# Turning queries and keys of self-attention: TensorE transposes against transposing DMA transfers

## Chip, cores and metric

The kernel runs on one core of a Trainium2 chip. The metric is the device time of one launch in microseconds, as the median of several runs. One execution is also taken by the hardware profiler; its page and its trace are what is read below. PE is TensorE (PEld its weight loads), DVE is VectorE, ACT is ScalarE, POOL is GpSimd, SP is SyncE, and SPq is SyncE's DMA queue.

## What is computed

Two decoder layers on x of shape (2, 1024, 256), with a context of 77 rows. The part that matters is layer 0's self-attention, with 16 heads of 16 channels:

```
q = quat_norm(quat_linear(x, qW, qb))
k = quat_norm(quat_linear(x, kW, kb))
v = quat_linear(x, vW, vb)
scores = einsum('bthd,bshd->bhts', q, k) * scale + mean(sin(J)) * 0.1
out = quat_linear(einsum('bhts,bshd->bthd', softmax(scores), v), oW, ob)
```

After it come a memory attention over the context, a feed-forward of 8 experts, and layer 1 (a long convolution, a cross-attention, and a feed-forward with quantised weights). Each is added to x and normalised.

## The kernel before

Each engine has its own instruction stream, written out by hand, with semaphores between them. The 2,048 rows are 16 tiles of 128 (T = 16, TB = 8 for each batch).

**Projections** (L853 to L882 on VectorE, L1386 to L1422 on TensorE). For each tile t, TensorE turns x and projects queries, keys and values. VectorE adds the bias (`biased`, L766), then, for a tile two steps back, takes the reciprocal of the norms and scales (`normed`, L773 and L775), and splits each value into a high and a low float16 part (`low_part`, L786 and L787). GpSimd adds pairs of squares and the bias of the values, and at the end a bias to x (L362).

**Self-attention** goes by UN = 16 units, each two heads of one batch. A unit has 8 steps `kt`, one for each tile of 128 keys. `stage(u)` on VectorE copies the unit's queries (L805) and keys (L810) out of QKH into QS and KS: 128 rows in partitions, and for each of 8 tiles 128 float16 values (2 heads x 4 parts x 16 channels). TensorE turns each tile (`turn_q`, L1331; `turn_k`, L1340) into bank 7, and VectorE copies the bank to QT and KT (`turned_q`, L820; `turned_k`, L824). QS, KS, QT and KT have two buffers each.

TensorE's order in a unit: at each step the next two `scores` (L1352; three ahead of the exponentials, in six banks), then `values` (L1366), then at steps 0 and 1 the turns of the next unit's queries, and at steps 3 and 4 those of its keys. ScalarE takes one exponential of 128x1024 for each `scores` (L518). VectorE's order in unit u (`attn_unit`): stage unit u+1, the two copies of turned tiles, in units 1 to 9 a part of the quantisation of the last weights (L834 to L840), then the copy of the unit's output out of bank 6 (L850). Unit 0's turns stand inside the projections, the queries' after tile 12 and the keys' after tile 14, and their copies at t = 14 and t = 15.

**SyncE** issues nearly all DMAs in one order. After the loads of the last weights it waits for each third of their quantisation, stores it to w_kept (L292), loads two experts (L284, L285), waits until the keys of the last unit are staged (L296), and then loads the weights of layer 1 (L298 and on).

Of the kernel before, what the change touches and what calls it, by code (L numbers as in the profile page):

```python
# [7 lines left out]
F16 = mybir.dt.float16  # L8
# [8 lines left out]
P = 128  # L17
B, L, D = 2, 1024, 256
T = B * L // P
TB = T // B  # L20
# [3 lines left out]
UN = B * NP  # L24
# [24 lines left out]

LN_CN = tuple(range(LN_C, LN_C + E - 2)) + (LN_C + E, LN_C + E + 3)  # L50
LN_DN = (LN_CN[6] - 2, LN_CN[6] - 1, LN_CN[7] - 2, LN_CN[7] - 1) + tuple(range(LN_CN[7] + 1, LN_E))

TURN_Q = {0: range(0, 4), 1: range(4, 8)}
TURN_K = {3: range(0, 4), 4: range(4, 8)}

UX = T * KD
AHEAD = 3
# [14 lines left out]
def decoder(nc, a, out):  # L72
    w_kept = nc.dram_tensor("w_kept", (P, 18, D), F32, kind="Internal").ap()
    with ExitStack() as ctx:
        sems = {}

        def sem(name):
            if name not in sems:
                sems[name] = ctx.enter_context(nc.semaphore(name))
            return sems[name]  # L80
# [171 lines left out]
        def bank(n, dt=F32):  # L252
            v = PS[:, n, :]
            return v if dt == F32 else v.bitcast(dt)
# [6 lines left out]
        def _(sp):  # L261
# [21 lines left out]
            def load_expert(e):  # L283
# [3 lines left out]
            sp.dma_start(wq[:, 6:12], a["L1_ffn_w_up"].rearrange("(k p) d -> p k d", p=P)).then_inc(sem("w_up_raw"), 16)  # L287
            sp.dma_start(wq[:, 12:18].rearrange("p (k c) d -> p k (c d)", k=KD),
                         a["L1_ffn_w_down"].rearrange("(k p) i -> p k i", p=P)).then_inc(sem("w_down_raw"), 16)
            for n in range(3):  # L290
                sp.wait_ge(sem("w_deq"), n + 1)
                sp.dma_start(w_kept[:, 6 * n:6 * n + 6], wq[:, 6 * n:6 * n + 6]).then_inc(sem("w_kept"), 16)  # L292
            sp.wait_ge(sem("w_kept"), 16 * 3)
            load_expert(0)
            load_expert(1)
            sp.wait_ge(sem("ks"), UN)  # L296
            for i, w in enumerate(("L1_attn_W_proj", "L1_xattn_Wq", "L1_xattn_Wk", "L1_xattn_Wv")):
                sp.dma_start(l1raw[i], a[w].rearrange("(k p) d -> p k d", p=P)).then_inc(sem("l1_w_in"), 16)  # L298
            for i, w in enumerate(("L1_attn_b_proj", "L1_attn_gamma", "L1_attn_beta", "L1_xattn_bo")):
# [422 lines left out]
        def _(dve):  # L722
# [69 lines left out]
            def stage(u):  # L792
                w = u % 2
                if u == 0:
                    dve.wait_ge(sem("j_exp"), 1)
                    dve.wait_ge(sem("const"), 9)
                    dve.wait_ge(sem("v_biased"), TB)
                    dve.wait_ge(sem("qk_lo"), TB)
                    for v in range(2):
                        ins = dve.tensor_scalar(VS[v][:, :, :, DH:DH + 1], ones[:, 0:1, None, None].to_broadcast([P, TB, 2, 1]), ec, None, ALU.mult)  # L800
                    link(ins)
                if u >= 2:
                    dve.wait_ge(sem("q_tr"), u - 1)
                for s in range(4):
                    ins = dve.tensor_copy(QS[w][:, :, :, s, :], QKH[:, 0, u, :, s // 2, :].rearrange("p t (h d) -> p t h d", h=2))  # L805
                ins.then_inc(sem("qs"), 1)
                if u >= 2:
                    dve.wait_ge(sem("k_tr"), u - 1)
                for s in range(4):
                    ins = dve.tensor_copy(KS[w][:, :, :, s, :], QKH[:, 1, u, :, s % 2, :].rearrange("p t (h d) -> p t h d", h=2))  # L810
                ins.then_inc(sem("ks"), 1)
                if u >= 2:
                    dve.wait_ge(sem("pv_done"), TB * (u - 1))
                dve.tensor_scalar(VS[w][:, :, :, 0:DH], VV[:, u].rearrange("p t (h d) -> p t h d", h=2), ec, None, ALU.mult).then_inc(sem("vs"), 1)

            def turned_q(u):
                dve.wait_ge(sem("q_tr"), u + 1)
                if u >= 2:
                    dve.wait_ge(sem("qk_done"), 2 * TB * (u - 1))
                dve.tensor_copy(QT[u % 2], bank(7, F16)).then_inc(sem("qt"), 1)  # L820

            def turned_k(u):
                dve.wait_ge(sem("k_tr"), u + 1)
                dve.tensor_copy(KT[u % 2], bank(7, F16)).then_inc(sem("kb"), 1)  # L824

            def quantised(n, part):

# [14 lines left out]
            def attn_unit(u):  # L842
                if u + 1 < UN:
                    stage(u + 1)
                    turned_q(u + 1)
                    turned_k(u + 1)
                if 1 <= u <= 9:
                    quantised((u - 1) // 3, (u - 1) % 3)
                dve.wait_ge(sem("pv_done"), TB * u + TB)
                dve.tensor_copy(OSB[:, u], bank(6)).then_inc(sem("o_evac"), 1)  # L850

            for t in range(T + 3):
                if t < T:  # L853
                    biased(t)
                if t == T - 2:
                    turned_q(0)
                if t == T - 1:
                    turned_k(0)
                if t == 4:
                    mask()  # L860

# [437 lines left out]
        def _(pe):  # L1299
# [22 lines left out]
                mm.then_inc(sem("v_mm"), 1)  # L1322


            def turn_q(u, tiles):
                if 0 in tiles:
                    pe.wait_ge(sem("qs"), u + 1)
                    if u >= 1:
                        pe.wait_ge(sem("kb"), u)
                for k in tiles:  # L1330
                    mm = pe.transpose(bank(7, F16)[:, P * k:P * k + P], QS[u % 2][:, k].rearrange("p h s d -> p (h s d)"), ident16)  # L1331
                if TB - 1 in tiles:
                    mm.then_inc(sem("q_tr"), 1)

            def turn_k(u, tiles):
                if 0 in tiles:
                    pe.wait_ge(sem("ks"), u + 1)
                    pe.wait_ge(sem("qt"), u + 1)
                for k in tiles:
                    mm = pe.transpose(bank(7, F16)[:, P * k:P * k + P], KS[u % 2][:, k].rearrange("p h s d -> p (h s d)"), ident16)  # L1340
                if TB - 1 in tiles:
                    mm.then_inc(sem("k_tr"), 1)

            def scores(n):

                u, kt, half = n // (2 * TB), n // 2 % TB, n % 2
                if n % (2 * TB) == 0:
                    pe.wait_ge(sem("kb"), u + 1)
                if n >= 3:
                    pe.wait_ge(sem("exp_done"), n - 2)  # L1350
                for h in range(2):
                    mm = pe.matmul(bank(2 * (n % 3) + h), KT[u % 2][64 * h:64 * h + 64, P * kt:P * kt + P],  # L1352
                                   QT[u % 2][64 * h:64 * h + 64, 512 * half:512 * half + 512], start=True, stop=True)
                mm.then_inc(sem("qk_done"), 1)
# [15 lines left out]
            def attn_unit(u):  # L1370
                for kt in range(TB):
                    for n in range(2 * (TB * u + kt) + 3, 2 * (TB * u + kt) + 5):
                        if n < 2 * TB * UN:
                            scores(n)
                    values(u, kt)
                    if u + 1 < UN:
                        if kt in TURN_Q:
                            turn_q(u + 1, TURN_Q[kt])
                        if kt in TURN_K:
                            turn_k(u + 1, TURN_K[kt])  # L1380


            x_turn(0)
# [2 lines left out]
            for t in range(T):  # L1386
# [29 lines left out]
                                           start=(k == 0), stop=(k == KD - 1))  # L1416
                    mm.then_inc(sem("mem_g_mm"), 1)

                if t == TB + 4:
                    turn_q(0, range(TB))  # L1420
                if t == T - 2:
                    turn_k(0, range(TB))  # L1422

            pe.wait_ge(sem("qk_biased"), T)
            pe.wait_ge(sem("v_evac"), T)
# [414 lines left out]
```

## Time and profile before

| | us |
|---|---|
| median of 3 runs | 878.62 (876.58 to 883.43) |
| the profiled execution, its own time | 880.1 |
| its span, first to last instruction | 878.3 |
| PE busy | 764.4 (87%) |
| ACT busy | 553.1 (63%) |
| DVE busy | 543.4 (62%) |
| POOL busy | 188.3 (21%) |
| mean granted TensorE clock | 0.951 of full speed |

The busy shares are over the whole span, and the stages differ. A busy PE is not PE at its peak: matmuls are pipelined, and their modelled ends overlap. The questions to ask of each stage are which engine has no gaps, and what the others wait for.

### The profile page before, as it was taken

To read this page: it belongs to the slowest core of one execution; us is meant where nothing else is said; L and a number is where in the kernel's file an instruction comes from. 1 tells how busy PE (TensorE), PEld (TensorE's weight loads), DVE (VectorE), ACT (ScalarE), POOL (GpSimd) and SP (SyncE) were. 2 spreads that over 40 slices of the span, in tenths; PEclk is the share of its full clock that TensorE was granted. 3 is DMA by queue.
4 is the path that set the end of the run, shared out by engine and by line. 5 is a ranking of instruction groups with operands and counts; after the bars stand their busy time and mean duration, and the time that the engine had idled before them with its cause. 6 is when DMAs were issued, how large, how long until landed. Compare 5 with 4: busy or idle time off the path is not lost.

```text
span 878.3 us, 11330 instructions
## 1 busy us (share of the span) xinstructions
PE 764.4 (87%) x4105; PEld 446.5 (51%) x4105; DVE 543.4 (62%) x1120; ACT 553.1 (63%) x941; POOL 188.3 (21%) x214
## 2 busy tenths in 40 slices
PE   4974899999999989999699999679899979994397
PEld 2642122222222228988588888346556844441286
DVE  4899334342412118869821647878977567898886
ACT  3555799999999981423221341475777533598991
POOL 1678000000000002306000402384544200000002
PEclk9997899999999999999899999889999989998599
DMA  7200000000150220202053200002000000000002
GB/s 204 91 0 1 1 1 37 1 37 1 42 188 1 70 69 1 96 1 97 1 192 114 78 1 1 0 1 72 10 28 1 1 1 0 1 0 0 1 24 72
DMA packets 23582, 33.76 MB, mean 38 GB/s; under 512 B 3074, under 2 KB 20328, under 8 KB 23400
## 3 DMA queue, kind: packets, MB, share of 16 engines
q1 hardware_dynamic: 23384, 32.92, 11.3%
q8 instruction: 33, 0.54, 0.3%
q14 instruction: 21, 0.17, 0.1%
q10 hardware_dynamic: 144, 0.13, 0.1%
HBM read 28.59 MB, written 4.46 MB: 38 GB/s over the span
## 4 chain that ended last, share of the span: by engine, by line
PE 39%; ACT 31%; DVE 21%; issue 6%; POOL 1%; SPq 1%; DMA 1%; DVEq 0%; POOLq 0%; ACTq 0%
ACT arena L518 24%; PE banks L1812 5%; PE banks L1804 5%; PE banks L1605 5%; PE banks L1593 5%; PE banks L1705 3%; PE banks L1677 2%; DVE arena L893 2%; DVE arena L901 2%; DVE arena L1185 2%; PE banks L1502 2%; DVE arena L773 1%; ACT arena L695 1%; ACT arena L681 1%; PE banks L1625 1%
## 5 line engine op out<-in xcount | busy, mean ns | idle before, releaser
L518 ACT ACTIVATE arena<-banks 128x1024 f32<-128x1024 f32 x256 | 236.3, 1060 | 10.0 <-PE banks L1352 7.5
L1366 PE MATMUL banks<-arena 128*32 128x512 f32 x1024 | 138.1, 611 | 2.3 <-ACT arena L518 0.8
L342 POOL TENSOR_SCALAR arena<-arena 128x2 f32<-128x2 f32 (+1 forms) x38 | 10.0, 263 | 474.1 <-DVE arena L896 474.1
L1352 PE MATMUL banks<-arena 64*128 64x512 f16 x512 | 89.3, 389 | 11.9 <-ACT arena L518 8.0
L1804 PE MATMUL banks<-arena 128*128 128x512 f32 x192 | 85.9, 610 | 3.8 <-DVE arena L1196 3.7
L609 ACT ACTIVATE arena<-banks,arena 128x77 f32<-128x77 f32 x256 | 58.9, 363 | 22.1 <-DVE arena L1109 22.1
L1352 PEld LDWEIGHTS banks<-arena 64*128 64x128 f16 x512 | 22.9, 93 | 95.9 <-ACT arena L518 78.1
L1812 PE MATMUL banks<-arena 128*128 128x256 f32 x192 | 44.5, 397 | 26.6 <-ACT arena L716 26.6
L1804 PEld LDWEIGHTS banks<-arena 128*128 128x128 f32 x192 | 37.4, 196 | 51.7 <-issue 48.7
L1605 PE MATMUL banks<-arena 128*128 128x256 f32 x256 | 58.1, 389 | 5.8 <-DVEq L1031 5.8
L1605 PEld LDWEIGHTS banks<-arena 128*128 128x128 f32 x256 | 49.9, 196 | 13.1 <-issue 6.2
L1593 PE MATMUL banks<-arena 128*128 128x256 f32 x256 | 56.2, 380 | 0.0
L1812 PEld LDWEIGHTS banks<-arena 128*128 128x128 f32 x192 | 38.5, 201 | 33.0 <-ACT arena L716 27.4
L421 POOL TENSOR_TENSOR arena<-arena 128x616 f32<-128x616 f32 x32 | 42.2, 1320 | 59.6 <-DVE arena L1117 59.5
L824 DVE COPY arena<-banks 128x1024 f16<-128x1024 f16 x16 | 11.0, 690 | 70.4 <-PE banks L1340 70.4
L901 DVE TENSOR_SCALAR arena<-arena 128x256 f32<-128x256 f32 x96 | 45.5, 527 | 13.1 <-POOL arena L344 13.0
L1677 PE MATMUL banks<-arena 128*128 128x308 f32 x128 | 43.1, 462 | 11.5 <-ACT arena L609 8.4
L1593 PEld LDWEIGHTS banks<-arena 128*128 128x128 f32 x256 | 48.7, 190 | 6.4
L579 ACT ACTIVATE arena<-banks,arena 128x256 f32<-128x256 f32 x64 | 26.2, 473 | 39.9 <-PE banks L1593 39.8
L850 DVE COPY arena<-banks 128x512 f32<-128x512 f32 x16 | 11.1, 691 | 64.7 <-PE banks L1366 64.7
L675 ACT ACTIVATE arena<-banks 128x512 f32<-128x512 f32 x48 | 28.1, 609 | 36.0 <-PE banks L1804 36.0
L535 ACT ACTIVATE arena<-banks 128x1024 f32<-128x1024 f32 x18 | 18.5, 1028 | 44.6 <-PE banks L1475 38.8
(221 smaller groups left out, 1407.4 us busy)
## 6 DMA issues: line engine op xcount, KB each, us to landing
arena<-in_L_ffn_w SPq DMA_DIRECT2D x16, 1024.0 KB, 7.4
w_kept<-arena SPq DMA_DIRECT2D x3, 768.0 KB, 3.3
arena<-w_kept SPq DMA_DIRECT2D x3, 768.0 KB, 5.1
arena<-in_x SPq DMA_DIRECT2D x4, 512.0 KB, 8.1
out_x<-arena SPq DMA_DIRECT2D x3, 512.0 KB, 2.9
arena<-in_L_ffn_b SPq DMA_DIRECT2D x1, 1024.0 KB, 9.0
arena<-in_L_ffn_w_gate SPq DMA_DIRECT2D x1, 768.0 KB, 7.4
arena<-in_L_ffn_w_up SPq DMA_DIRECT2D x1, 768.0 KB, 9.1
```

The costliest lines, as they stand in the source:

```text
L421: pool.tensor_tensor(Ex[n % 4], Ex[n % 4], rdx[:, n % 4, :, None].to_broadcast([P, HC, LC]), ALU.mult).then_inc(sem("xa_w"), 1)
L518: act.activation(PT[kt % 2][:, half], PS[:, 2 * (n % 3):2 * (n % 3) + 2, :], ACT.Exp, scale=DH ** -0.5 / QK_UP ** 2).then_inc(sem("exp_don ...
L609: ins = act.activation(Ex[n % 4][:, h, :], PS[:, 2 * (n % 2) + h // 4, LC * (h % 4):LC * (h % 4) + LC], ACT.Exp, scale=-1.0, bias=mxs[:, 8 ...
L675: act.activation((GF if n < IC * G4 else UF)[:, c, 512 * g:512 * g + 512], bank(2 + n % 4), ACT.Copy).then_inc(sem("gu"), 1)
L901: ins = dve.tensor_scalar(dst(j), src(j), mv[:, at + j, 0:1], rstd[:, at + j:at + j + 1], ALU.subtract, ALU.mult)
L1352: mm = pe.matmul(bank(2 * (n % 3) + h), KT[u % 2][64 * h:64 * h + 64, P * kt:P * kt + P], QT[u % 2][64 * h:64 * h + 64, 512 * half:512 * h ...
L1366: mm = pe.matmul(PS[32 * j:32 * j + 32, 6, :], VS[w][:, kt, h, :], PT[kt % 2][:, half, h, :], start=(kt == 0), stop=(kt == TB - 1))
L1593: mm = pe.matmul(PS[:, f // 2, 256 * (f % 2):256 * (f % 2) + 256], W1r[r][:, k, P * f:P * f + P], XT[:, k, TE * P * e:TE * P * e + TE * P] ...
L1605: mm = pe.matmul(bank(4 + e % 2)[:, D * j:D * j + D], hT[e % 2][:, f, P * j:P * j + P], W2r[r][:, f, :], start=(f == 0), stop=(f == FT - 1))
L1677: mm = pe.matmul(PS[:, 2 * (n % 2) + q, 0:4 * LC], qTx[g % 2][:, k, P * j:P * j + P], Kbd[:, k, g // 2, 4 * q:4 * q + 4, :].rearrange("p h ...
L1804: mm = pe.matmul(bank(2 + n % 4), (wgT if n < IC * G4 else wuT)[:, k, P * c:P * c + P], XT[:, k, 512 * g:512 * g + 512], start=(k == 0), s ...
L1812: mm = pe.matmul(PS[:, t % 8 // 2, D * (t % 2):D * (t % 2) + D], UF[:, c, P * t:P * t + P], wdT[:, c, :], start=(c == 0), stop=(c == IC - 1))
```

## The change

The turns on TensorE and the copies out of bank 7 go. In their place SyncE issues two DMA transfers a unit, SBUF to SBUF, that transpose: QS to QT and KS to KT, 128 x 1024 float16 each. For unit u it waits until queries are staged, until the transfer of the unit before has landed, and until the scores of unit u-2 are done; then, after the first is issued, until keys are staged. TensorE waits for both transfers (of 16 counts each) ahead of the first scores of a unit. VectorE waits for the transfer of unit u-2, where it waited for its turns, before it writes the staging buffer again. SyncE's stores to w_kept stand behind the transfers of units 5, 8 and 11, and the loads of experts 0 and 1 behind those of unit 12. The loads of layer 1's weights wait until the last transfers have landed.

```diff
-            for n in range(3):
-                sp.wait_ge(sem("w_deq"), n + 1)
-                sp.dma_start(w_kept[:, 6 * n:6 * n + 6], wq[:, 6 * n:6 * n + 6]).then_inc(sem("w_kept"), 16)
-            sp.wait_ge(sem("w_kept"), 16 * 3)
-            load_expert(0)
-            load_expert(1)
-            sp.wait_ge(sem("ks"), UN)
+            def turned(u):
+
+                sp.wait_ge(sem("qs"), u + 1)
+                if u >= 1:
+                    sp.wait_ge(sem("q_turned"), 16 * u)
+                if u >= 2:
+                    sp.wait_ge(sem("qk_done"), 2 * TB * (u - 1))
+                sp.dma_start(QT[u % 2].rearrange("p (k n) -> p k n", k=TB), QS[u % 2].rearrange("p k h s d -> p k (h s d)"),
+                             transpose=True).then_inc(sem("q_turned"), 16)
+                sp.wait_ge(sem("ks"), u + 1)
+                if u >= 1:
+                    sp.wait_ge(sem("k_turned"), 16 * u)
+                sp.dma_start(KT[u % 2].rearrange("p (k n) -> p k n", k=TB), KS[u % 2].rearrange("p k h s d -> p k (h s d)"),
+                             transpose=True).then_inc(sem("k_turned"), 16)
+
+            for u in range(UN):
+                turned(u)
+                if u in (5, 8, 11):
+                    n = (u - 5) // 3
+                    sp.wait_ge(sem("w_deq"), n + 1)
+                    sp.dma_start(w_kept[:, 6 * n:6 * n + 6], wq[:, 6 * n:6 * n + 6]).then_inc(sem("w_kept"), 16)
+                if u == 12:
+                    sp.wait_ge(sem("w_kept"), 16 * 3)
+                    load_expert(0)
+                    load_expert(1)
+            sp.wait_ge(sem("q_turned"), 16 * UN)
+            sp.wait_ge(sem("k_turned"), 16 * UN)
...
                 if u >= 2:
-                    dve.wait_ge(sem("q_tr"), u - 1)
+                    dve.wait_ge(sem("q_turned"), 16 * (u - 1))
...
                 if u >= 2:
-                    dve.wait_ge(sem("k_tr"), u - 1)
+                    dve.wait_ge(sem("k_turned"), 16 * (u - 1))
...
-            def turned_q(u):
-                dve.wait_ge(sem("q_tr"), u + 1)
-                if u >= 2:
-                    dve.wait_ge(sem("qk_done"), 2 * TB * (u - 1))
-                dve.tensor_copy(QT[u % 2], bank(7, F16)).then_inc(sem("qt"), 1)
-
-            def turned_k(u):
-                dve.wait_ge(sem("k_tr"), u + 1)
-                dve.tensor_copy(KT[u % 2], bank(7, F16)).then_inc(sem("kb"), 1)
...
                     stage(u + 1)
-                    turned_q(u + 1)
-                    turned_k(u + 1)
...
-                if t == T - 2:
-                    turned_q(0)
-                if t == T - 1:
-                    turned_k(0)
...
                 if n % (2 * TB) == 0:
-                    pe.wait_ge(sem("kb"), u + 1)
+                    pe.wait_ge(sem("q_turned"), 16 * u + 16)
+                    pe.wait_ge(sem("k_turned"), 16 * u + 16)
...
                     values(u, kt)
-                    if u + 1 < UN:
-                        if kt in TURN_Q:
-                            turn_q(u + 1, TURN_Q[kt])
-                        if kt in TURN_K:
-                            turn_k(u + 1, TURN_K[kt])
...
-                if t == TB + 4:
-                    turn_q(0, range(TB))
-                if t == T - 2:
-                    turn_k(0, range(TB))
```

The functions `turn_q` and `turn_k` on TensorE go with them.

## Rows read from the trace of the kernel before

**Rows 1.** Busy time of each engine in three stretches; here self-attention (stretch, length, engines).
```profile
79.00:327.00 248.00, 230.50 (x1770) 57.13 (x1770) 79.71 (x204) 236.86 (x258) 9.04 (x4) 0.97 0.12 40
```

**Rows 2.** Chain of waits in self-attention (start us, length us, what).
```profile
104.65 1.70 ACT arena L518 x2
...
178.37 1.70 ACT arena L518 x2
...
311.05 1.70 ACT arena L518 x2
...
323.80 2.10 ACT arena L518 x2
```

**Rows 3.** Timeline of ACT in unit 0 (start us, length us; in brackets idle before, releaser).
```profile
79.60 3.75 ACT L518 ACTIVATE arena<-banks 128x1024 f32<-128x1024 f32 x4
84.17 1.02 ACT L518 ACTIVATE arena<-banks 128x1024 f32<-128x1024 f32 x1 [0.83 <-PE banks L1366]
92.69 1.02 ACT L518 ACTIVATE arena<-banks 128x1024 f32<-128x1024 f32 x1 [7.49 <-PE banks L1352]
95.07 2.02 ACT L518 ACTIVATE arena<-banks 128x1024 f32<-128x1024 f32 x2 [1.35 <-PE banks L1366]
97.39 2.85 ACT L518 ACTIVATE arena<-banks 128x1024 f32<-128x1024 f32 x3 [0.30 <-PE banks L1366]
```

**Rows 4.** Timeline of all engines, unit 0 and a step of unit 6.
```profile
90.81 0.63 DVE L805 COPY arena<-arena 128x256 f16<-128x256 f16 x4
91.36 0.62 DVE L810 COPY arena<-arena 128x256 f16<-128x256 f16 x4
...
91.50 0.61 PE L1331 MATMUL banks<-arena 128*128 128x128 f16 x4 [7.46 <-DVE arena L805]
...
93.00 1.94 PE L1366 MATMUL banks<-arena 128*32 128x512 f32 x8
...
182.28 0.61 PE L1352 MATMUL banks<-arena 64*128 64x512 f16 x4
182.82 1.06 PE L1366 MATMUL banks<-arena 128*32 128x512 f32 x8
```

**Rows 5.** Timeline of DVE in the projections: the bias additions.
```profile
53.34 0.68 DVE L766 TENSOR_TENSOR arena<-banks,arena 128x512 f32<-128x512 f32 x1
...
56.66 0.68 DVE L766 TENSOR_TENSOR arena<-banks,arena 128x512 f32<-128x512 f32 x1
...
62.39 0.67 DVE L766 TENSOR_TENSOR arena<-banks,arena 128x512 f32<-128x512 f32 x1
...
73.34 0.68 DVE L766 TENSOR_TENSOR arena<-banks,arena 128x512 f32<-128x512 f32 x1
```

**Rows 6.** A stretch of 3 us in unit 0; the granted clock stands third from last.
```profile
92.00:95.00 3.00, 3.00 (x16) 0.47 (x15) 0.25 (x1) 1.02 (x1) 0.00 (x0) 0.50 0.01 3
```

**Rows 7.** Timeline of DVE after the start of unit 6.
```profile
180.12 0.69 DVE L850 COPY arena<-banks 128x512 f32<-128x512 f32 x1 [2.42 <-PE banks L1366]
180.72 0.62 DVE L805 COPY arena<-arena 128x256 f16<-128x256 f16 x4
181.26 0.63 DVE L810 COPY arena<-arena 128x256 f16<-128x256 f16 x4
```

**Rows 8.** Small loads: SP's timeline, DMA issues (KB, us to landing), queue from 4 to 6.
```profile
0.79 1.39 SPq L264 DMA_DIRECT2D arena<-in_L_attn_qW  x2
...
4.85 1.27 SPq L264 DMA_DIRECT2D arena<-in_L_attn_oW  x2
...
arena<-in_L_attn_oW SPq DMA_DIRECT2D x2, 64.0 KB, 2.4
...
q1 hardware_dynamic: 863, 0.21, 45.6%
```

**Rows 9.** DMA issues from 180 to 350 us: KB each, median us to landing.
```profile
arena<-in_L_ffn_w SPq DMA_DIRECT2D x4, 1024.0 KB, 9.9
...
arena<-in_L_attn_W_proj SPq DMA_DIRECT2D x1, 256.0 KB, 2.9
```

More of the change, by code:

```diff
@@ L51 @@
 LN_DN = (LN_CN[6] - 2, LN_CN[6] - 1, LN_CN[7] - 2, LN_CN[7] - 1) + tuple(range(LN_CN[7] + 1, LN_E))
-TURN_Q = {0: range(0, 4), 1: range(4, 8)}
-TURN_K = {3: range(0, 4), 4: range(4, 8)}
 UX = T * KD
@@ L1322, in project @@
                 mm.then_inc(sem("v_mm"), 1)
[L1325 to L1342, printed above, removed]
             def scores(n):
```

## Prediction

> **What bounds the kernel now.** I read the busy shares by stage first. Self-attention runs from 79 to 327 us; ScalarE is busy in 236.9 of its 248.0 us, PE in 230.5, VectorE in 79.7 [rows 1]. Its work is 256 exponentials, 16 a unit (L518). The chain of waits stands on them from start to start: the pair at 104.65 opens unit 1, the pair at 178.37 unit 6, and the pair at 311.05 unit 15, which is 14.74 us a unit [rows 2]. Unit 15, in which PE turns nothing, has its eight pairs from 311.05 to 323.80 in seven steps, 12.75 us, so 14.57 us a unit [rows 2]. ScalarE's timeline then shows where it stands idle: only in unit 0, for 0.83, 7.49, 1.35 and 0.30 us, 9.97 in all [rows 3]. The long one is the thing to see. PE stands at its first turn of unit 1 (L1331) until VectorE has staged queries (L805, ending at 91.44); the next scores are queued behind that turn, so ScalarE gets no banks to read [rows 4]. VectorE is late because it still finishes the projections.
>
> **What goes.** In units 1 to 14, 16 turns each leave PE, and two copies out of bank 7 leave VectorE. The turns made ScalarE's pace 14.74 instead of 14.57, so (14.74 - 14.57) x 14 = 2.4 us come back. The copies lie beside ScalarE's work and give nothing themselves.
>
> In the projections VectorE sets the pace: three of its bias additions L766 follow that of 62.39 by 73.34, 3.65 us each, against 3.32 undisturbed (53.34 to 56.66) [rows 5]. The excess of 1.0 us is unit 0's turns and the copy L820, so the last bias addition comes 1.0 us earlier, and the first exponential at 78.6 instead of 79.60. VectorE itself gains the second copy as well, 0.6 us by the bank copy L850, next of kin [rows 7], which puts the staging of unit 1 at 89.84 (queries) and 91.98 - 1.6 = 90.38 (keys) [rows 4].
>
> The 7.49 us wait goes, since PE no longer waits for staging in the middle of unit 0. PE remains cold at that point. After the idle stretch eight value matmuls took 1.94 us against 1.06 later [rows 4]; the granted clock there was 0.50, which is 1.2 GHz, against a mean of 0.97 over the stage, nearly always 2.4 GHz [rows 1, 6]. So I keep 1.5 of the other 2.48 us. The earliest start of unit 1 is 78.6 + 14.57 + 1.5 = 94.7, a gain of 10.0 against 104.65.
>
> **What comes.** Each unit has two transfers of 256 KB on SyncE's queue. PE waits for both in front of the first scores of the unit, and behind that wait are queued the values of step 6 and two more pairs of scores. After landing, ScalarE needs one pair of scores and one step of values: 0.6 + 1.1 = 1.7 us [rows 4]. In a running unit, VectorE first copies the output of the last one (L850, 180.12), then has queries staged at 181.34 and keys at 181.89, which is 2.97 and 3.52 us after the unit's start at 178.37 [rows 2, 7]. Queries cannot be staged earlier, since that copy stands ahead of them. So with a fixed latency F and a time T in the DMA engines for each transfer, a unit lasts at least 2.97 + F + 2T + 1.7. The bar is 14.74.
>
> F: 64 KB in 256 pieces of 256 bytes land 2.4 us after issue [rows 8]. In a stretch of only such pieces 863 took 45.6% of 16 engines x 2 us, so 16.9 ns each in one engine [rows 8], and 256 of them 0.27 us. I take F = 2.0, rounded down from 2.1. The bar is then passed at T = 4.0.
>
> T: no row shows a transposing transfer. Its source is 1,024 runs of 256 bytes. If it moves like a plain one, T is 1,024 x 16.9 / 16 ns = 1.1 us. If every value is written on its own, it is 131,072 x 16.9 / 16 ns = 138 us. These are the two ends. Neither is likely: neighbours in a source row go to different partitions, which speaks against the first, and the second is a hundred times the price of any row. With no row nearer to either, I take the geometric middle, 12.2 us, pieces of some 11 values. Pieces of 16 values would give 8.7.
>
> The Trainium skill, page "VectorE: DVE Perf Modes", section "The three transpose paths", gives 1309 ns for one 128x128 turn by DMA against 390 ns on TensorE. Eight such blocks are, as an estimate, 10.5 us, and the sum below would give 1094. No run so far shows either figure.
>
> With T = 12.2 the first keys land at 89.84 + 2.0 + 24.4 = 116.2 and unit 1 starts at 117.9, 13.3 late. PE has then been idle and is cold, for which I add the restart stalls of 1.35 + 0.30 = 1.65 [rows 3]: 14.9. The following 14 starts are 2.97 + 2.0 + 24.4 + 1.7 + 1.65 = 32.7 us apart, 18.0 over 14.74, or 252. The gain of 2.4 and the start's 10.0 are swallowed by it. Sum: 880.1 + 14.9 + 252 = 1147 against the profiled execution's own time; that one lies 1.5 us above the median of 878.62, so **1146**.
>
> **Edits that I cost at nothing.** The stores to w_kept move behind the turns of units 5, 8 and 11; nobody waits for them but the expert loads. These four loads of 1 MB land after 9.9 us at the median [rows 9] and are issued behind the turns of unit 12. On a 14.7 us unit they are over before unit 13's turns. At 32.7 us the more so. If they overlapped they would add up to 10 us once. The eleven loads of layer 1's weights now wait for the last turns. None is larger than an expert's, their readers come after attention, and unit 15's own 14.57 us cover them.
>
> **Rivals.** *One: transfers as quick as plain ones.* A 256 KB load landed in 2.9 us [rows 9], so keys could land 0.54 + 2.9 after queries are staged, at 93.3. The eight 64 KB loads, 2,048 pieces of 256 bytes like one unit's two transfers, took 7.1 us from 0.79 to about 7.9, which puts it at 96.9 [rows 8]. Both lie within the 14.74 of a running unit, and then nothing waits after unit 1; that holds up to T = 4.0. Midway, 5.3 us, unit 1 starts at 96.8, 7.8 earlier than before; with the 2.4 it is 10.2, so 869.9 profiled and 868.4. The ends are 866 and, without the 2.4, 873. For it speaks that every row of the queue shows quick pieces; against, that no row shows a value leaving its run. The Trainium skill, page "Advanced Engine Details and Errata", section "X-Bar Transpose (TRN2)", says that transposing DMAs are as fast as regular ones, which is this rival; the trace so far has none to hold beside it.
>
> *Two: a price for each block.* If each of the 16 blocks of 128x128 costs what a small DMA costs in the queue, 7.1 / 8 = 0.89 us [rows 8], keys land 14.2 us after queries are staged. Unit 1 then starts at 89.84 + 14.2 + 1.7 + 1.65 = 107.4, 2.7 late, and the other 14 starts are 20.5 us apart, 5.8 over: 81. That is 880.1 + 84 - 1.5 = 963. For it: SyncE was held 0.6 to 0.7 us for each small load [rows 8]. Against: 256 KB in one piece landed in 2.9 us, hardly later than 64 KB in 2.4 [rows 8, 9], so bytes or blocks cost little there.
>
> *Three: the cold clock alone.* PE loses the turns and may be granted less in running units. Unit 15 speaks against it: without turns it kept its pace. It is in the range of rival one.
>
> **How the numbers follow.** Forecast (T above 7.3, times from 1000 on) 0.45; rival two and T between 4 and 7.3 together 0.18; rival one 0.37. One per cent is 8.8 us, about what can be told from no change: below 869.8 is faster. Of rival one's 0.37 I put 0.23 below it and 0.14 within; slower gets 0.63. The forecast's own range is 1000 to 1250: T = 15.7, some nine values to a piece. It reaches no further, since 0.12 is left above. As cases of both signs hold most of the chance, the range for 8 in 10 has to take in rival one from 866: **866 to 1250**.
>
> **What would show it.** Right: in the list of waits ScalarE's L518 waits for scores (L1352) or values (L1366) 15 times, some 18 us at a time; PE's granted clock is near 0.5 after each; PE's scores wait for a DMA from arena to arena; the landing time of the second transfer of a unit is about 26 us. Right in any case: the 7.49 us wait is gone and the first exponential starts near 78.6. Wrong: a landing time of both below 9 us from the staging of queries, starts of units 14.6 us apart, unit 1 starting near 97. If landing is short but SyncE's own issue is long, T is the sequencer's and not the engines'; the sum is the same.

## The result: one per cent faster, where 30% more time was forecast

The changed kernel takes **869.8 us** (median of 12 runs, 868.4 to 873.9) against 879.1 of the kernel before beside it (12 runs, 876.3 to 884.0). The ratio is 0.9899, with a 95% interval of 0.9885 to 0.9913. The prediction said 1146 and slower. What happened is its first rival, which gave 868.4, and 869.9 for the profiled execution; that took 869.56 around a span of 867.8.

ScalarE's timeline in unit 0 answers to [rows 3] (start, length, in brackets the idle time before it and its releaser; L535 is the line L518 of before, L1349 the values L1366, L1335 the scores L1352):

```profile
77.89 3.75 ACT L535 ACTIVATE arena<-banks 128x1024 f32<-128x1024 f32 x4
82.45 1.94 ACT L535 ACTIVATE arena<-banks 128x1024 f32<-128x1024 f32 x2 [0.82 <-PE banks L1349]
85.29 9.27 ACT L535 ACTIVATE arena<-banks 128x1024 f32<-128x1024 f32 x10 [0.90 <-PE banks L1349]
95.89 16.61 ACT L535 ACTIVATE arena<-banks 128x1024 f32<-128x1024 f32 x18 [1.32 <-PE banks L1349]
```

The wait of 7.49 us is gone. The two waits for values that stood around it are now 0.82 and 0.90, and one is new, 1.32 us where unit 1 starts. After that row ScalarE runs through. The busy time of the page by line says the same for all 256 exponentials (busy, mean ns, then idle before and its releaser):

```profile
L535 ACT ACTIVATE arena<-banks 128x1024 f32<-128x1024 f32 x256 | 235.4, 1094 | 3.1 <-PE banks L1349 3.0
```

The timeline of all engines shows the new path, where [rows 4] had a turn on PE waiting for VectorE's copies:

```profile
89.13 0.64 DVE L822 COPY arena<-arena 128x256 f16<-128x256 f16 x4
...
89.68 0.63 DVE L827 COPY arena<-arena 128x256 f16<-128x256 f16 x4
89.79 1.23 SPq L294 DMA_TRANSPOSE arena<-arena  x1
...
91.12 1.27 SPq L299 DMA_TRANSPOSE arena<-arena  x1
...
94.37 0.39 PE L1335 MATMUL banks<-arena 64*128 64x512 f16 x2 [1.71 <-DMA arena<-arena]
```

Queries are staged at 89.77, their transfer holds SyncE's queue for 1.23 us, the keys' transfer follows, and PE's first scores of unit 1 go 4.6 us after the staging. The chain of waits puts a length on the keys' transfer, 3.15 us (start, length, what):

```profile
91.12 3.15 DMA arena<-arena
94.28 0.09 issue
94.37 0.39 PE banks L1335 x2
94.76 1.04 PE banks L1349 x8
```

In the DMA view of 98 to 118 us, four transfers of running units (packets, MB, share of 16 engines; then the issues with the median us to landing):

```profile
q1 hardware_dynamic: 4224, 1.05, 27.4%
...
arena<-arena SPq DMA_TRANSPOSE x4, 3.2
```

A transfer is 1,056 packets. 27.4% of 16 engines x 20 us over 4,224 packets is 20.8 ns each, so a transfer keeps the 16 engines for 1,056 x 20.8 / 16 ns = 1.37 us. This is the prediction's T, for which it took 12.2.

**Where the 10.5 us of the profiled spans went** (878.3 to 867.8). From the bias addition of 56.66 [rows 5] to the first exponential it was 22.94 us and is now 22.06 (55.83 to 77.89): 0.9. The first exponential came 1.7 earlier, so the other 0.8 lies ahead of those tiles, in a stretch that the change does not touch. Unit 0 lasted 25.05 us (79.60 to 104.65) and lasts 18.00: 7.05. Units 1 to 14 took 206.4 [rows 2] and take 205.6 (95.89 to 301.48): 0.8. Unit 15 is the same, seven steps in 12.75 us (the chain: 301.48 to 314.23). After attention 552.4 us became 551.5, which lies within the 550.1 to 553.0 of the other kernels here. What the change can claim of it is 0.9 + 7.05 + 0.8, some 8.8, beside 9.3 between the medians.

### The profile page after: what moved, and what is told of

Same layout as the page of the kernel before. It is cut to its first block, busy times and chain, and to the rows that moved or that the text cites. A ratio compares the mean times of both kernels' runs of the same rounds, so it can differ in the third digit from the quotient of the medians.

```text
span 867.8 us, 10805 instructions
## 1 busy us (share of the span) xinstructions
PE 752.1 (87%) x3849; PEld 431.9 (50%) x3849; DVE 522.2 (60%) x1088; ACT 552.0 (64%) x941; POOL 191.5 (22%) x214
## 4 chain that ended last, share of the span: by engine, by line
PE 38%; ACT 30%; DVE 21%; issue 7%; DMA 1%; SPq 1%; POOL 1%; DVEq 0%; POOLq 0%; ACTq 0%
ACT arena L535 24%; PE banks L1786 5%; PE banks L1778 5%; PE banks L1579 5%; PE banks L1567 5%; PE banks L1679 3%; PE banks L1651 2%; DVE arena L894 2%; DVE arena L902 2%; DVE arena L1186 2%; PE banks L1476 2%; DVE arena L790 2%; ACT arena L712 1%; ACT arena L698 1%; PE banks L1599 1%
## 5 line engine op out<-in xcount | busy, mean ns | idle before, releaser
L535 ACT ACTIVATE arena<-banks 128x1024 f32<-128x1024 f32 x256 | 235.4, 1094 | 3.1 <-PE banks L1349 3.0
L1349 PE MATMUL banks<-arena 128*32 128x512 f32 x1024 | 138.1, 611 | 2.2 <-ACT arena L535 0.8
L1335 PE MATMUL banks<-arena 64*128 64x512 f16 x512 | 99.4, 390 | 23.1 <-ACT arena L535 9.4
L359 POOL TENSOR_SCALAR arena<-arena 128x2 f32<-128x2 f32 (+1 forms) x38 | 12.7, 334 | 462.2 <-DVE arena L897 462.2
L1335 PEld LDWEIGHTS banks<-arena 64*128 64x128 f16 x512 | 24.7, 93 | 166.8 <-ACT arena L535 154.4
L1786 PEld LDWEIGHTS banks<-arena 128*128 128x128 f32 x192 | 38.4, 200 | 33.1 <-ACT arena L733 27.4
L894 DVE BATCH_NORM_STATS2 arena<-arena 128x6 f32<-128x256 f32 x112 | 40.2, 414 | 1.2
```

The costliest lines, as they stand in the source:

```text
L535: act.activation(PT[kt % 2][:, half], PS[:, 2 * (n % 3):2 * (n % 3) + 2, :], ACT.Exp, scale=DH ** -0.5 / QK_UP ** 2).then_inc(sem("exp_don ...
L894: ins = dve.bn_stats(bstat[:, at + j, :], view(j))
L1349: mm = pe.matmul(PS[32 * j:32 * j + 32, 6, :], VS[w][:, kt, h, :], PT[kt % 2][:, half, h, :], start=(kt == 0), stop=(kt == TB - 1))
L1786: mm = pe.matmul(PS[:, t % 8 // 2, D * (t % 2):D * (t % 2) + D], UF[:, c, P * t:P * t + P], wdT[:, c, :], start=(c == 0), stop=(c == IC - 1))
```

## The experiments

Two questions were open. Does the gain need the DMA at all, or is it only the end of PE's wait in unit 0 (theory A), against work taken off PE and VectorE in every unit (theory B)? And what do the transfers cost, by which the prediction fell? Medians, ratios to the kernel before on the same chip and what ScalarE did in attention (from the first exponential to the end of the last, and idle within it, from its timeline):

| kernel | us | ratio, 95% interval | attention | idle | unit 1 starts after the first exponential |
|---|---|---|---|---|---|
| before | 879.1 | 1 | 246.3 | 9.97 | 25.05 |
| changed | 869.8 | 0.9899 (0.9885 to 0.9913) | 238.4 | 3.04 | 18.00 |
| turns of unit 1 later, all on PE | 869.9 | 0.9898 (0.9878 to 0.9918) | 238.4 | 2.13 | 17.19 |
| GpSimd later, kernel before | 871.3 | 0.9918 (0.990 to 0.9935) | 239.6 | 3.38 | |
| both of these, no DMA | 869.9 | 0.9903 (0.9882 to 0.9924) | 238.0 | 1.76 | 16.81 |
| GpSimd later, changed kernel | 870.5 | 0.9890 (0.9865 to 0.9914) | 237.0 | 1.72 | |
| staging earlier, kernel before | 876.7 | 0.9968 (0.9957 to 0.998) | 244.1 | 7.32 | |
| **staging earlier, changed kernel** | **867.9** | 0.9879 (0.986 to 0.9898) | 236.1 | 0.82 | |
| DMA in units 0 and 1 only | 874.0 | 0.9935 (0.9917 to 0.9953) | 240.6 | 4.21 | 18.48 |
| DMA in all but unit 0 | 872.7 | 0.9921 (0.9902 to 0.9939) | 239.8 | 4.18 | 19.14 |
| plain copies in place of transposing | 870.5 | 0.9893 (0.9872 to 0.9914) | 237.7 | 2.40 | 17.26 |
| three more transfers a unit | 882.8 | 1.0045 (1.002 to 1.007) | 251.0 | 14.35 | |
| six more transfers a unit | 969.0 | 1.1010 (1.0991 to 1.1029) | 339.4 | 98.8 | |
| each transfer in eight pieces | 1077.4 | 1.2245 (1.2216 to 1.2275) | 441.9 | 201.7 | |

### Where the gain is: parts of the change alone

**Two units by DMA.** The changed kernel, with the turns of units 2 to 15 back on PE and their copies on VectorE:

```diff
+DMA_UNITS = (0, 1)
...
-                turned(u)
+                if u in DMA_UNITS:
+                    turned(u)
...
+                    if u + 1 < UN and u + 1 not in DMA_UNITS:
+                        if kt in TURN_Q:
+                            turn_q(u + 1, TURN_Q[kt])
...
```

> Units 0 and 1 turned by DMA, units 2 to 15 by TensorE as before. Theory A, the gain is the end of TensorE's in-order wait in unit 0 and a shorter tail of the projections: first exponential at 77.9, unit 1 starts near 95.9, units 14.74 apart again, which gives back the 0.8 us of the 14 later units; ratio to before 0.989 to 0.992, some 871. Theory B, the gain is work taken off TensorE and VectorE in every unit: 14 of 16 units have it back, so 2 of 16 of 9.3 us are left, some 878, ratio 0.998 to 1.000.

Measured 874.0, ratio 0.9935: 5.1 of the 9.3 us with 2 of 16 units. That lies between theory A's 871 and theory B's 878, in neither range of ratios. The start is as the changed kernel's (22.04 us from the bias addition to the first exponential). The waits at unit 1 are 1.88 and 0.70 instead of 1.32 alone; the idle time of attention is 1.2 us more, its busy rest 1.0 us more. That is 2.2 of the 4.8 us between the profiled spans (872.6 and 867.8). Of the others, 1.5 lie ahead of the same bias addition (57.36 instead of 55.83) and 1.1 behind attention; the edit touches neither stretch, and the cause of that part is open.

**All but unit 0 by DMA.** The same edit with `DMA_UNITS = tuple(range(1, UN))`.

> Unit 0 turned by TensorE inside the projections as before, units 1 to 15 by DMA. Theory A: the first exponential is back at 79.6 from 77.9, and 1.7 us are given back: some 871.5, ratio 0.991 to 0.993. Theory B: 15 of 16 units keep the gain, 0.6 us are given back: some 870.4.

Measured 872.7, ratio 0.9921: within theory A's range of ratios, and 1.2 over its 871.5. From the bias addition to the first exponential it is 22.95 us again, where the kernel before has 22.94 and the changed one 22.06: unit 0's turns by DMA are worth the 0.9 us of the projections' tail, as the prediction had it (1.0). The wait at unit 1 is 2.92 us here, 1.6 more than in the changed kernel. Another 1.1 us lie ahead of that bias addition (56.94 instead of 55.83), where the edit changes nothing.

**Turns of unit 1 later, no DMA.** The kernel before, PE turning everything; only in unit 0 it turns unit 1's queries after step 4 and its keys after step 5, when VectorE has staged them:

```diff
+TURN_Q0, TURN_K0 = {4: range(0, 8)}, {5: range(0, 8)}
...
-                        if kt in TURN_Q:
-                            turn_q(u + 1, TURN_Q[kt])
-                        if kt in TURN_K:
-                            turn_k(u + 1, TURN_K[kt])
+                        q_at, k_at = (TURN_Q, TURN_K) if u else (TURN_Q0, TURN_K0)
+                        if kt in q_at:
+                            turn_q(u + 1, q_at[kt])
+                        if kt in k_at:
+                            turn_k(u + 1, k_at[kt])
```

> The kernel before, all turns on TensorE; only the turns of unit 1 stand later in TensorE's order, queries' after step 4 and keys' after step 5 of unit 0. Theory A (the gain is the end of an in-order wait): ScalarE's 7.49 us at exponential 5 is gone; TensorE waits about 1 us for the queries at 91.4 and then for two copies out of bank 7, unit 1 starts at 96.5 to 98 instead of 104.65, total 871 to 873, ratio 0.991 to 0.993. Theory B (work taken off TensorE and VectorE in every unit): no gain, 879. Theory C, from the early staging on the kernel before, which gave 2.4 of 7.5: VectorE's copies out of bank 7 stand behind its tail and hold TensorE anyway; they come after 91.98, so here they cost 2 to 3 us, 873 to 875.

Measured 869.9, 1 us under theory A's 871 to 873 and **the changed kernel's time without a DMA**. ScalarE's timeline of it:

```profile
84.22 1.94 ACT L519 ACTIVATE arena<-banks 128x1024 f32<-128x1024 f32 x2 [0.82 <-PE banks L1367]
86.69 9.37 ACT L519 ACTIVATE arena<-banks 128x1024 f32<-128x1024 f32 x10 [0.53 <-PE banks L1367]
96.84 15.69 ACT L519 ACTIVATE arena<-banks 128x1024 f32<-128x1024 f32 x17 [0.78 <-PE banks L1367]
```

The wait of 7.49 is gone here too, by a move in the order of PE's instructions. This shows that the wait was one of order: unit 1's turns stood ahead of scores of unit 0 that needed nothing of them.

### Why VectorE was late

VectorE's timeline of the kernel before, ahead of the staging of [rows 4], beside GpSimd's:

```profile
78.52 2.07 DVE L775 TENSOR_TENSOR arena<-arena 128x512 f32<-128x512 f32 x1
80.52 2.57 DVE L786 CAST arena<-arena 128x512 f16<-128x512 f32 x1
83.12 2.72 DVE L787 TENSOR_TENSOR arena<-arena 128x512 f16<-128x512 f32 x1
...
88.51 0.41 DVE L786 CAST arena<-arena 128x512 f16<-128x512 f32 x1
88.96 0.69 DVE L787 TENSOR_TENSOR arena<-arena 128x512 f16<-128x512 f32 x1
```

GpSimd's timeline of the same kernel:

```profile
77.71 10.33 POOL L362 TENSOR_TENSOR arena<-arena 128x1024 f32<-128x1024 f32 x4
```

The same cast takes 2.57 us while GpSimd adds x + bo, and 0.41 after it; the same addition 2.72 and 0.69.

**GpSimd later.** The kernel before, with one wait in front of GpSimd's four additions, until keys of unit 1 are staged:

```diff
+            pool.wait_ge(sem("ks"), 2)
```

> The kernel before; only GpSimd's addition of the output bias to x (four of 2.6 us) waits until unit 1 is staged. VectorE's tail of the projections then runs alone: five operations that took 2.07, 2.50, 2.73, 1.66 and 0.95 us take 0.4 to 1.2, some 5 us less, and queries are staged at 86 to 87. Theory A: TensorE's wait in unit 0 shrinks from 7.49 to some 2.5, total 874, ratio 0.994. If GpSimd's additions only move and slow VectorE's work of unit 1 as much, nothing is lost, since that is off the path. Theory B: nothing, 879.

Measured 871.3, where theory A expected 874. VectorE begins to stage queries 4.7 us after the first exponential, not 11.2, and PE's wait is nearly gone (ScalarE's timeline):

```profile
84.15 1.02 ACT L519 ACTIVATE arena<-banks 128x1024 f32<-128x1024 f32 x1 [0.97 <-PE banks L1353]
86.53 1.94 ACT L519 ACTIVATE arena<-banks 128x1024 f32<-128x1024 f32 x2 [1.35 <-PE banks L1367]
88.70 23.98 ACT L519 ACTIVATE arena<-banks 128x1024 f32<-128x1024 f32 x26 [0.23 <-PE banks L1367]
```

ScalarE waits 0.97 us for those scores, where 2.5 was expected. So the wait of 7.49 us had two conditions, GpSimd's additions that made VectorE late and PE's order that made lateness cost something. Taking away either brings nearly all of it.

**Both, without a DMA**: the later turns (queries after step 3, keys after 5) and GpSimd's wait together.

> TensorE turns all units; both orders are mended (unit 1's turns after steps 3 and 5, GpSimd's addition behind the staging of unit 1). Theory A: neither wait is left, unit 1 starts at 96 or before; what the transfers still have over it is 0.9 us of the projections' tail and 0.8 to 1.7 us of pace over 14 units: 870.5 to 872. Theory B: 878 to 879.

Measured 869.9, a little under theory A's 870.5 to 872 and no less than with the turns alone: the two take away the same wait.

**GpSimd later in the changed kernel**, by the same line.

> The changed kernel with GpSimd's addition moved in the same way. Theory A: queries are staged 5 us earlier, at 85 instead of 89.8, both transfers have landed at 89.5, before TensorE comes to the first scores of unit 1, and the remaining wait of 1.32 us goes: 868.5, ratio 0.988, as the early staging gave. If unit 1's own work on VectorE suffers from GpSimd: its transfers are issued later and up to 2 us come back.

Measured 870.5. The wait of 1.32 us at unit 1 is gone and attention is 1.4 us shorter in the profile, but the medians do not tell it from the changed kernel (869.8), and its interval (0.9865 to 0.9914) holds the expected 0.988 as well.

**Staging earlier, kernel before.** VectorE stages unit 1 before it finishes the last tiles of the projections:

```diff
+                if 1 <= u and u + 1 < UN:
+                    stage(u + 1)
                 if u + 1 < UN:
-                    stage(u + 1)
                     turned_q(u + 1)
...
+                if t == T - 1:
+                    stage(1)
```

> The kernel before, with nothing moved but the staging of unit 1, which VectorE now does at the end of the loop step of the last tile, ahead of the last two normalisations; TensorE turns all units. Theory A: the wait of 7.49 us is gone without any DMA, first exponential at 79.6 as before, unit 1 starts at 96 to 98 instead of 104.65, total 870.5 to 873, ratio 0.990 to 0.993. Theory B: all turns and copies are still there, so no gain, 879. A third way: staging there delays VectorE's tail by 1.6 us and this delays ScalarE, then 872.5 to 875.

Measured 876.7, where theory A expected 870.5 to 873: a miss. VectorE's timeline shows why:

```profile
79.99 7.39 DVE L805 COPY arena<-arena 128x256 f16<-128x256 f16 x4
87.30 2.80 DVE L810 COPY arena<-arena 128x256 f16<-128x256 f16 x4
```

The four staging copies that take 0.63 us in [rows 4] take 7.39 beside GpSimd's additions, which run from 80.34 to 89.61 there. Moved ahead they meet GpSimd, and the copies out of bank 7 come behind VectorE's remaining work, for which PE waits 2.98 us. Idle time falls from 9.97 to 7.32 only. The first exponential also comes 23.9 us after the bias addition (58.30 to 82.23) and not 22.9, so a part of the third way, VectorE's tail delayed by the staging, is there too.

**Staging earlier, changed kernel.** The same edit.

> The changed kernel with the staging of unit 1 at the same early place. Theory A: the transfers of unit 1 land well before its scores, the remaining wait of 1.3 us for them goes, unit 1 starts near 94.6, total 868.5, ratio to before 0.988, and 1.3 us below the changed kernel. Theory B: nothing, 869.8.

Measured 867.9, the lowest median of all, where theory A expected 868.5. The staging copies are just as slow (four of them, L827 at 76.78, last 7.16 us), but PE's order does not hang on them as long as the transfers land within unit 0, and ScalarE does not wait at unit 1 (its timeline; the second row runs past it):

```profile
76.33 3.75 ACT L535 ACTIVATE arena<-banks 128x1024 f32<-128x1024 f32 x4
80.91 32.28 ACT L535 ACTIVATE arena<-banks 128x1024 f32<-128x1024 f32 x35 [0.82 <-PE banks L1351]
```

It beats the kernel before clearly; its interval overlaps that of the changed kernel, so 1.9 us between those two is what the medians say and not more.

### What a transfer costs

**Plain copies.** The changed kernel without `transpose=True` on both transfers, the layout of the destination as it was. It leaves out the turning, so its scores are of unturned data, and only its time is read:

> The changed kernel with plain copies of QS to QT and KS to KT in place of the transposing ones; the scores are of unturned data, and the exponentials' inputs are other numbers of the same size. Theory Q, a transposing transfer costs about what a plain one of as many bytes does: lands in 2.2 to 3.0 us, SyncE held 0.4 to 0.5 us, unit 1 starts up to 1.3 us earlier than in the changed kernel. If turning costs the engines, their time for each transfer falls from some 1.4 us by much.

Measured 870.5 (2 runs), ratio 0.9893, the changed kernel's time. In the same stretch of 20 us with four transfers:

```profile
q1 hardware_dynamic: 576, 1.05, 14.0%
...
arena<-arena SPq DMA_DIRECT2D x4, 256.0 KB, 2.3
```

14.0% against 27.4%: a plain transfer keeps the engines 0.70 us and a transposing one 1.37. It lands 2.3 us after issue instead of 3.2, and holds SyncE 0.47 to 0.55 us instead of 1.23 to 1.29. All that is close to what was expected, and for the kernel's time it is nothing, since it lies within what a running unit leaves. At unit 1 ScalarE still waits 1.58 us. The keys had landed at about 95.3 there (92.93 + 2.4), and PE's first scores went at 96.19, so landing sooner does not by itself end that wait.

**In eight pieces.** Each transfer is cut into eight of one block of 128x128:

```diff
+                for c in range(8):
+                    tiles = slice(TB // 8 * c, TB // 8 * c + TB // 8)
+                    sp.dma_start(QT[u % 2].rearrange("p (k n) -> p k n", k=TB)[:, tiles], QS[u % 2].rearrange("p k h s d -> p k (h s d)")[:, tiles],
+                                 transpose=True).then_inc(sem("q_turned"), 16)
```

> Each transposing transfer cut into eight of one 128x128 block. It tells what of SyncE's 1.23 us is for each transfer and what for each block: if for each block (0.15 us), eight of them hold SyncE 1.3 to 2 us and little changes; if for each transfer (0.4 to 1.2 us at least, as other issues), eight hold it 4 to 10 us, keys land 9 to 20 us after queries are staged, and the kernel is slower: unit 1 later by 6 to 16 us, and beyond 10 us of landing time each unit longer: 876 to 1030.

Measured 1077.4 (2 runs), above the 876 to 1030 that was expected. SyncE's timeline at unit 1:

```profile
90.23 10.02 SPq L296 DMA_TRANSPOSE arena<-arena  x8
100.35 10.10 SPq L303 DMA_TRANSPOSE arena<-arena  x8
```

Ten us for eight pieces is 1.25 each (1.09 to 1.23 and a gap of 0.04 by the chain of waits), the same 1.23 that one transfer of all eight blocks takes. **The hold is a price for each transfer, and not for each block or byte.** Had the change been written with a transfer for each block, it would have been slower by 22%. That is the kind of rival two, which gave 963: it took 0.89 us a block. The chain of waits shows what the last piece of unit 3's keys releases:

```profile
165.96 2.37 DMA arena<-arena
...
168.42 0.61 PE banks L1339 x2
169.03 1.86 PE banks L1353 x8
```

Units 2 and 3 start at 143.85 and 171.02, 27.2 us apart: 3.1 until queries are staged, 19.0 until SyncE has sent the first fifteen pieces, 2.4 until the last has landed, and 2.7 until ScalarE starts. So SyncE's queue sets the pace here. It is the case that the prediction named at its end, in which T is the sequencer's and not the engines'.

**More transfers.** Three (then six) more transposing transfers of the queries go into spare buffers, between the queries' and the keys':

```diff
+                for i in range(3):
...
+                    sp.dma_start(SPARE[(3 * u + i) % 2].rearrange("p (k n) -> p k n", k=TB), QS[u % 2].rearrange("p k h s d -> p k (h s d)"),
+                                 transpose=True).then_inc(sem(f"spare{(3 * u + i) % 2}"), 16)
```

> The changed kernel with three more transposing transfers of the same 256 KB in each unit, into spare buffers, between that of the queries and that of the keys. Theory Q (a transfer costs its queue 1.3 us and lands 3.2 us after issue, as the trace of the changed kernel shows): keys land some 4 us later than now; unit 1 starts 4 us later; in running units they land at 4.5 + 4 = 8.5 us after queries are staged, ahead of the 10.0 us at which they are needed, so nothing more: 874. Theory S (the step of the prediction: 12 us in the engines for each): 36 us more in each unit, over 1300.

Measured 882.8, about 9 over what was expected. ScalarE's timeline of it, at units 1 and 2:

```profile
102.27 15.05 ACT L543 ACTIVATE arena<-banks 128x1024 f32<-128x1024 f32 x16 [6.99 <-PE banks L1359]
117.64 8.36 ACT L543 ACTIVATE arena<-banks 128x1024 f32<-128x1024 f32 x9 [0.32 <-PE banks L1359]
```

SyncE's timeline of it, for unit 2:

```profile
105.46 1.23 SPq L295 DMA_TRANSPOSE arena<-arena  x1
106.74 6.12 SPq L300 DMA_TRANSPOSE arena<-arena  x3
112.96 1.28 SPq L305 DMA_TRANSPOSE arena<-arena  x1
```

The row of 6.12 us is not three long holds. Each of the three holds SyncE 1.2 to 1.3 us like a lone one, and ahead of the third SyncE waits 2.2 us until the first has landed and its spare buffer is free, which takes 4.87 us here and 3.2 to 3.3 at unit 1; why it landed so late is open. The keys go out at 112.96 and land 3.08 later, at 116.0. Queries were staged at 105.42, so that is 10.6 us. The prediction's bar leaves 14.74 - 2.97 - 1.7 = 10.1 from staging to landing, and unit 2 starts 0.32 us late. In unit 3 the keys go out at 126.43, so they land 9.1 us after staging, and ScalarE does not wait. **The bar holds**; only what was held against it was wrong. The other long waits are 6.99 us at unit 1, which has less slack, and 3.34 us at unit 13, beside the loads of the experts' weights; 0.92 and 0.17 at units 6 and 10 are small.

> Six more transposing transfers in each unit. Theory Q: keys land 8 us later (1.33 us each), 12.5 us after queries are staged, 2.5 us past the need, in each of 15 units, and TensorE may turn cold: unit 1 starts 8 us later, each other unit 2.5 to 4 us longer: 870 + 8 + 14 x 2.5 to 4 = 913 to 934. If spare buffers are waited for, each costs up to 1.6 us and it is 936 to 960. Theory S: over 1800.

Measured 969.0, above either range expected (913 to 934, and 936 to 960 with waits for the spare buffers, which it has). From unit 2 on every unit waits:

```profile
129.04 1.94 ACT L543 ACTIVATE arena<-banks 128x1024 f32<-128x1024 f32 x2 [6.03 <-PE banks L1359]
131.38 13.13 ACT L543 ACTIVATE arena<-banks 128x1024 f32<-128x1024 f32 x14 [0.40 <-PE banks L1359]
150.42 15.07 ACT L543 ACTIVATE arena<-banks 128x1024 f32<-128x1024 f32 x16 [5.91 <-PE banks L1359]
```

Units 2 and 3 are 21.4 and 19.8 us long (129.04, 150.42, 170.22), with a second, shorter wait behind most of the long ones: the regime that the forecast described. Its mechanism exists; it takes eight transfers a unit to reach it, not two.

## Why the prediction was wrong, step by step

**The failing step is T**, the time of a transposing transfer in the DMA engines. The prediction found no row for it, bounded it by 1.1 us (moves like a plain one) and 138 us (every value on its own), and took the geometric middle, 12.2. Measured it is 1.37, next to the lower end. The argument was that neighbours of a source row go to different partitions, "which speaks against the first"; but a transfer is 1,056 packets of some 250 bytes (1.05 MB in 4,224), the size of the source's runs, and each takes 20.8 ns against 16.9 for a plain one [rows 8]. It doubles a plain SBUF copy (0.70) mostly by its number of packets: the plain one has 144 a transfer, and at 16.9 ns each 1,056 packets would take 1.12 us. So what the prediction had as F + 2T, 26.4 us from staging to landing, was 4.4 (1.33 until the second issue, 3.1 until it lands) against a bar of 10.1, and the term of 252 us is zero. The kernel therefore moved the other way, and the median lies near the low end of the range of 866 to 1250, where rival one had put it. A geometric middle between ends a hundred apart is no reading of a row; the one nearest row of size, 256 KB in 2.9 us [rows 9], differed from what was measured (3.1 to 3.3) by 0.2 to 0.4.

**F** was right: 2.0 taken, 3.15 - 1.37 = 1.8 measured.

**The Trainium skill's 1309 ns** for a turn of 128x128 ("VectorE: DVE Perf Modes", "The three transpose paths"), which the prediction multiplied by eight: the trace has a figure of that size, the hold of 1.23 to 1.29 us at the median, but for a transfer, of 32 KB or 256 KB alike. The multiplication was the error, though the sum did not rest on it. **That transposing DMAs are as fast as regular ones** (the Trainium skill, "Advanced Engine Details and Errata", "X-Bar Transpose (TRN2)"): by the engines' time they are not (1.37 against 0.70), nor by landing (3.2 against 2.3) or hold; by the kernel's time they are, 869.8 and 870.5.

**The 7.49 us wait goes**: right, and with it most of the result. Of the other 2.48 us, 1.5 were kept; 1.72 are there, and 1.32 of waiting for the transfer besides. Unit 0 was to last at least 16.1 us (78.6 to 94.7), and 18.2 by rival one (78.6 to 96.8); it lasts 18.00. VectorE's lateness was put down to the projections' work alone; the runs with GpSimd moved show that its length comes from GpSimd's additions beside it.

**The cold clock** was right up to the restart, and its end was not foreseen. A stretch of 3 us of the changed kernel (granted clock third from last):

```profile
83.00:86.00 3.00, 3.00 (x18) 0.49 (x20) 2.86 (x3) 2.10 (x3) 3.00 (x2) 0.60 0.00 0
86.00:89.00 3.00, 2.87 (x22) 0.45 (x14) 2.93 (x5) 3.00 (x5) 0.35 (x1) 1.00 0.00 0
```

Without the wait PE has the full clock, 2.4 GHz, from 86 us on; the kernel before stood at 0.50 still at 92 to 95 [rows 6].

**The first exponential 1.0 earlier**: right, 0.9, and shown by giving it back (all but unit 0).

**The pace of running units, 2.4 us**: mis-sized, 0.8. The prediction took unit 15's 14.57 for all; units 1 to 14 now last 205.6 / 14 = 14.69. Attention less its idle time is 236.2 to 236.4 in the kernels that turn on PE (before, later turns, GpSimd later, both; 236.8 with staging earlier) and 235.3 to 235.4 in those that turn by DMA (changed, and with GpSimd later or staging earlier), so 0.9 us is what removing 224 turns brings. What keeps running units 0.1 us over unit 15 is open.

**Edits costed at nothing** cost nothing that shows: no wait of ScalarE after unit 1 in the changed kernel. But the experts' loads were not over before unit 13's turns, as the prediction had it: its two transfers landed after 4.1 and 3.9 us instead of 3.2.

**Rivals.** One came true: 869.9 profiled where 869.56 was measured, unit 1 at 96.8 where it starts at 95.89. Within it the pace was 1.6 us too good, which unit 1 (0.9 earlier) and the stretch after attention (0.9 shorter) made up; that the total came out within 0.4 us is luck. Two is true in kind of the code split in pieces, at 1.25 us a block. Three did not come: the mean granted clock went from 0.951 to 0.958.

## What to carry to other kernels

Look first for what blocks an engine's queue in order: here a move of sixteen turns by a few steps bought as much as taking the turns off PE (869.9 and 869.8), and one wait on a neighbour that slows the late engine nearly as much (871.3). Of the 8.8 us that the DMA transfers gave, 7.05 were that one wait. They cost nothing in the running units, where their landing stayed under a bar that can be worked out from the trace before. Where no row shows an operation's price, write down the price at which the answer turns (here 4.0 us), weigh the two sides of that point by the nearest row, and don't take a middle between far ends.

## What the runs showed of the hardware

- A transposing SBUF transfer of 128x1024 f16 is 1,056 packets of 20.8 ns each in one engine, lands 3.2 us after issue, and holds the issuing queue 1.23 us, at 32 KB as at 256 KB. In a row, each holds it 1.2 to 1.3 us as well.
- Four f16 copies of 128x256 on VectorE take 0.63 us alone and 7.39 us beside GpSimd's four f32 additions, a factor of 12; a cast from f32 to f16 0.41 and 2.57, an addition 0.69 and 2.72. Three of the four copies take 2.38 us instead of 0.22, beside GpSimd additions of 2.35 each; the cast and the second addition come near the 2.6 (10.33 / 4) of those beside them. Each grows to about the length of one of GpSimd's additions, however short it is itself, as if it waited for one to end; the reciprocal of the same stretch (128x128, one operand) stays at 0.95. The Trainium skill, "SBUF — State Buffer", section "SBUF: two separate sides", calls the port pair that VectorE and GpSimd share "an exclusive lock, not a bandwidth split", held for the whole instruction and taken by a VectorE instruction with two SBUF operands or in a fast mode. The trace agrees: the additions with two operands in SBUF are hit, and the reciprocal with one is not. That the copies and casts run in a fast mode no row here shows, and no run tells the lock from another cause of such waits.
